# Window attention of a vision tower: the query and key product goes behind the projection, the value product changes its PSUM bank, and VectorE adds up rows earlier

## The reference, cut to what matters

```
xw  = windows of 8 x 8 = 64 positions, 64 channels each
qkv = xw @ qkv_w.T + qkv_b            # 8 heads of 8 channels
q, k = rope2(q), rope2(k)             # rotate pairs of channels by row and column
attn = softmax(q * 8 ** -0.5 @ k.T)   # 64 x 64, for each window and head
h = (attn @ v) @ proj_w.T + proj_b    # back in picture order
```

## Time and profile before

| | us |
|---|---|
| median of 3 runs | 1657.8 (1657.18 to 1657.87) |
| the profiled execution's own time | 1655.28 |
| its span in the trace | 1653.5 |
| TensorE busy, whole span | 1506.6 (91%) |
| VectorE busy | 1201.7 (73%) |
| ScalarE busy | 1004.9 (61%) |
| GpSimd busy | 614.9 (37%) |
| 8x8 stage, first to last transposition of maxima (L693) | 29.85 to 294.24 |

### The profile page before, as it was taken

One profiled execution on the slowest core, in us unless ns is written; L12 is line 12 of the kernel. 1 busy time (PEld: TensorE's weight loads), 2 busy tenths in 40 slices (PEclk: granted clock), 3 DMA queues, 4 the chain that ended last, 5 costly groups with the idle time before them and its releaser, 6 DMA issues.

```text
span 1653.5 us, 85382 instructions
## 1 busy us (share of the span) xinstructions
PE 1506.6 (91%) x30734; PEld 1082.0 (65%) x30734; DVE 1201.7 (73%) x3605; ACT 1004.9 (61%) x1925; POOL 614.9 (37%) x926
## 2 busy tenths in 40 slices
PE   6999999789999999999857999999999999999996
PEld 4777777668888888777745656556565655656552
DVE  2566666458888888888647778787787777877872
ACT  2444444345555555455312788888888888888876
POOL 4352232356666666666532222222222222222210
PEclk9999999989999999999976999999999999999996
DMA  5322222144444444444411454555545455554543
GB/s 140 69 50 48 47 47 42 46 119 124 129 126 128 134 129 124 129 128 127 115 38 33 73 93 81 85 87 80 92 79 90 82 84 88 78 93 78 90 81 57
DMA packets 146868, 147.44 MB, mean 89 GB/s; under 512 B 54898, under 2 KB 102258, under 8 KB 146546
## 3 DMA queue, kind: packets, MB, share of 16 engines
q1 hardware_dynamic: 137922, 117.38, 37.7%
q10 hardware_dynamic: 8880, 29.16, 6.1%
HBM read 66.48 MB, written 16.99 MB: 50 GB/s over the span
## 4 chain that ended last, share of the span: by engine, by line
PE 77%; ACT 9%; issue 6%; SPq 3%; POOL 2%; DVE 1%; DMA 1%; ACTq 0%; POOLq 0%; DVEq 0%
PE ps_D L923 10%; PE ps_D L831 8%; PE ps_OT L850 5%; ACT prob L1227 4%; PE ps_AV L942 4%; PE ps_AV L858 4%; PE ps_D L706 3%; ACT prob L1125 3%; PE ps_D L827 3%; PE ps_J L1000 3%; PE ps_J L1034 2%; PE ps_OT L1010 2%; PE ps_J L985 2%; PE ps_J L1065 2%; PE ps_OT L784 2%
## 5 line engine op out<-in xcount | busy, mean ns | idle before, releaser
L1227 ACT ACTIVATE prob<-ps_D 128x1024 bf16<-128x1024 f32 x448 | 459.4, 1028 | 114.8 <-PE ps_D L923 114.3
L1197 ACT ACTIVATE prob<-ps_D 100x512 f32<-100x512 f32 x256 | 138.8, 594 | 102.8 <-PE ps_D L831 102.8
L577 POOL TENSOR_TENSOR tile_a<-q_st,q_mask 128x512 f32<-128x512 f32 x128 | 135.2, 1056 | 150.7 <-PE ps_D L831 140.1
L831 PE MATMUL ps_D<-tile_a,key_patch 64*100 64x128 f32 x2048 | 174.6, 290 | 0.0
L1388 DVE TENSOR_REDUCE m_sb<-ps_D 128x4 f32<-128x400 f32 x256 | 134.5, 565 | 25.5 <-PE ps_D L808 25.5
L1350 DVE TENSOR_REDUCE top<-ps_D 128x8 f32<-128x512 f32 x128 | 79.6, 683 | 95.8 <-PE ps_D L684 95.7
L551 POOL TENSOR_TENSOR rstd_bin<-veps_bin,minus_half 128x2 f32<-128x2 f32 x64 | 44.1, 689 | 263.0 <-DVE veps_bin L1288 263.0
L551 POOL TENSOR_TENSOR rstd_ret<-veps_ret,minus_half 128x2 f32<-128x2 f32 x64 | 47.3, 739 | 241.8 <-DVE veps_ret L1288 241.8
L831 PEld LDWEIGHTS ps_D<-tile_a,key_patch 64*100 64x100 f32 x2048 | 134.0, 167 | 0.0
L827 PE MATMUL ps_D<-mT,key_rows 64*100 64x128 bf16 x1024 | 119.7, 229 | 6.3 <-ACT prob L1197 4.6
L923 PE MATMUL ps_D<-tile_b,w_parts 64*64 64x256 bf16 x2048 | 104.3, 287 | 15.5 <-ACT prob L1227 11.8
(11 more groups left out here) (184 smaller groups left out, 3828.4 us busy)
## 6 DMA issues: line engine op xcount, KB each, us to landing
tile_a<-xg SPq DMA_DIRECT2D x192, 128.0 KB, 4.5
tile_b<-xg SPq DMA_DIRECT2D x192, 128.0 KB, 4.5
key_st<-k_d SPq DMA_DIRECT2D x128, 162.0 KB, 3.1
tile_b<-v_d ACTq DMA_DIRECT2D x128, 120.0 KB
tile_b<-v_d ACTq DMA_DIRECT2D x64, 160.0 KB
w_exp<-experts SPq DMA_DIRECT2D x64, 129.0 KB, 2.3
xT<-in_x SPq DMA_DIRECT2D x32, 256.0 KB, 2.7
tile_a<-rot SPq DMA_DIRECT2D x256, 16.0 KB
```

Of the source, the lines that this page charges most:

```text
L577: gp.tensor_tensor(q_block[:, par, :].rearrange("c (p h q) -> c p h q", h=NH, q=NQ)[:, own, :, :], q_st[:, par, :].rearrange("c (p a q) -> ...
L831: mm = pe.matmul(s_loc[x][0:NKL, u * P:(u + 1) * P], key_patch[rows_of(x), par, at * NKL:(at + 1) * NKL], q_block[rows_of(x), par, at * P: ...
L1197: act.activation(prob1[0:NKL, 2 * g + x, :], s_loc[x][0:NKL, :], ACT.Exp).then_inc(T2["exp_done"], 1)
L1227: act.activation(sgn[:, k % 4, :], unit(k, par)[:, :], ACT.Sign).then_inc(BN["sign"], 1)
```

## The change

Four edits, all in the 8x8 stage:

- TensorE issues `tok_qk(i + 2)` behind `tok_project(i - 1)`, where it was ahead of `tok_scores(i)`.
- ScalarE issues `tok_sin(i + 2)` behind the four exponentials, where it was ahead of them.
- The values are made in columns 256 to 511 of bank OT, which the projection uses too, and no longer in bank T. With that the waits change: `tok_qk` no longer waits for `v_sb`. `tok_v` waits for `h_done` (VectorE's read of OT) in place of `cos_mul`. `tok_project` waits for `v_sb` (ScalarE's read of OT) too.
- VectorE issues `tok_rows(i - 1)` right behind `tok_normalize(i - 1)`, where it was behind the reductions.

```diff
             def tok_qk(...):
                 pe.wait_ge(T1["sin_in"], times(i))
-                pe.wait_ge(T1["v_sb"], times((i - 1) * 4))
             def tok_v(i, par):
                 pe.wait_ge(T1["v_sb"], times(i * 4))
-                pe.wait_ge(T1["cos_mul"], times(i + 2, NT))
+                pe.wait_ge(T1["h_done"], times(i - 1))
...
-                            at = (p * 2 + ab) * 32
-                            mm = pe.matmul(bank["T"][rows_of(e), at:at + 32], ...)
+                            at = 256 + (p * 2 + ab) * 32
+                            mm = pe.matmul(bank["OT"][rows_of(e), at:at + 32], ...)
             def tok_project(i):
                 pe.wait_ge(T1["attn_out"], times(i + 1))
+                pe.wait_ge(T1["v_sb"], times((min(i + 2, NT) if isinstance(i, int) else i + 2) * 4))
                 pe.wait_ge(T1["h_done"], times(i))
...
                 tok_top(i)
-                if not last or i + 2 < NT:
-                    tok_qk(i + 2, j + 1, par)
                 tok_scores(i, par)
                 if not last or i:
                     tok_project(i - 1)
+                if not last or i + 2 < NT:
+                    tok_qk(i + 2, j + 1, par)
...
             def tok(j, par):                          # ScalarE
-                if not last or i + 2 < NT:
-                    tok_sin(i + 2)
                 act.wait_ge(T1["av_done"], times(i))
                 act.wait_ge(T1["scores"], times(i + 1))
                 for n in range(4):
                     act.activation(prob1[:, n, :], s_tok[n][:, :], ACT.Exp).then_inc(T1["exp_done"], 1)
+                if not last or i + 2 < NT:
+                    tok_sin(i + 2)
...
                     tok_normalize(i - 1)              # VectorE
+                if not last or i:
+                    tok_rows(i - 1)
                 if not last or i + 2 < NT:
                     tok_rope(i + 2, par)
                 if not last or i + 1 < NT:
                     tok_max(i + 1)
-                if not last or i:
-                    tok_rows(i - 1)
```

More of the change, by code:

```diff
@@ L669, in tok_v @@
                         for e in range(2):
-                            at = (p * 2 + ab) * 32
-                            mm = pe.matmul(bank["T"][rows_of(e), at:at + 32], xT[rows_of(e), par, window(ab, p)], w_v1[rows_of(e), 32 * e:32 * (e + 1)],
+                            at = 256 + (p * 2 + ab) * 32
+                            mm = pe.matmul(bank["OT"][rows_of(e), at:at + 32], xT[rows_of(e), par, window(ab, p)], w_v1[rows_of(e), 32 * e:32 * (e + 1)],
                                            start=True, stop=True)
@@ L1105, in tok_v @@
                         act.activation(v_tok[par][rows_of(e), :, ab, :, at:at + HD],
-                                       bank["T"][rows_of(e), 0:256].rearrange("k (p s h d) -> k p s h d", p=4, s=2, d=HD)[:, :, ab, :, :], ACT.Copy).then_inc(T1["v_sb"], 1)
+                                       bank["OT"][rows_of(e), 256:512].rearrange("k (p s h d) -> k p s h d", p=4, s=2, d=HD)[:, :, ab, :, :], ACT.Copy).then_inc(T1["v_sb"], 1)
             def tok_sin(i):
```

## The result

| | before | after |
|---|---|---|
| median of the runs | 1657.74 (4 runs) | 1711.27 (4 runs, 1706.41 to 1716.79) |
| ratio, 95% interval | | 1.0296 (1.0261 to 1.033) |
| span of the profiled execution | 1653.5 | 1704.6 |
| first top (L693 before, L692 after) | 29.85 | 31.25 |
| top 7 | 93.57 | 101.70 |

The kernel is 3.0% slower. I had forecast 1680, slower, and a range up to 1702: the direction was right, the size less than half, and the time lies 9 us above the range. Of the 51.1 us between the spans, 1.4 are lost ahead of the first top, 6.7 until top 7, 40.8 in the 24 steps to top 31, and 2.2 behind them. So the loss is where I put it, and the question is why a step takes 10.06 and not 9.2. The profiled execution took 1706.4, the least of the four; the other three had a mean granted clock of 0.938 to 0.943, against 0.954 in this one.

What follows compares the result with a forecast made beforehand. TensorE's list and VectorE's chain were taken to bound steps of 8.36 us almost together. Late keys make it 9.2: +20.1 over 24 steps, +2.2 head, 1655.3 to 1677.6, plus 2.5 for the median: 1680, range 1664 to 1702.

Steps and rivals of the forecast that it cites:

- The copy of the maxima: Between top and scores: ScalarE's copy loses its cover, scores start at 0.77, 0.47 us of new idle time, step 8.68.
- The keys: Rotation and key transfers start later, so the second half of the maxima's products waits until 16.0; two steps take 18.4.
- The landing: From the eighth key issue's start to TensorE going on: 2.2 us, read from tile 0 only.
- The sum: 24 steps of 9.2 against 200.7 before: +20.1; with +2.2 for the head +22.3, so 1677.6, median 1680.
- The first rival: Keys late and the clock falls as well, in 10 of 24 steps at 1.9 us: 1699; chance 0.22.
- the step that fell before: Step 4 before the change: idle 1.07 and 0.57 came ahead of a 1.2 GHz stretch; one fall priced at 1.9.
- about 0.75 in each step: TensorE's stall for late keys ahead of the second half of the maxima's products, paid in full in every step.
- other steps of the head kept their clock: In the stage's first steps, an idle 1 us left the clock up; cited against the rival with clock falls.
- The head of the stage: Steps until tile 7, with constant loads between the keys in SyncE's queue: top 7 at 95.8, +2.2 us.
- Bank and rows at nothing: Values in the projection's bank and rows earlier cost nothing; the query and key product covers VectorE's addition, else 0.7 a step.
- Only the exposed copy: Rival: only the maxima's copy is exposed, keys in time, steps of 8.68 to 8.90: 1666 to 1671; chance 0.16.
- TensorE's list decides: Rival: reductions end 0.4 sooner, keys in time, steps of 8.40 on average: 1655 to 1658; chance 0.08.

Runs made afterwards that it cites:

- e2: Changed kernel with four key transfers per tile in place of eight (keys of every second head left out, output not the reference's): 1687.2 us, before 1659.1.
- e5: Changed kernel with half of the key transfers and one filler matmul on each side of the transposition of the maxima: 1662.1 us, before 1660.6.
- e10: Changed kernel with the last four key transfers of a tile issued by GpSimd and a filler matmul on each side of the transposition: 1663.4 us, before 1662.9.
- e3: Changed kernel with tok_sin, ScalarE's copy of bank J1, between the second and third exponential: 1688.8 us, before 1659.1.
- e6: Changed kernel, all keys, with three filler matmuls between the halves of the maxima's products and one on each side of the transposition: 1676.5 us, before 1660.6.
- e9: Changed kernel, all keys, with one filler matmul on each side of the transposition and none between the product halves: 1705.8 us, before 1662.9.
- e7: Changed kernel with query and key product and tok_sin moved back; values stay in bank OT, rows behind the division: 1691.9 us, before 1660.6.
- e8: Kernel before with only the addition of rows moved behind the division: 1735.1 us, ratio 1.0445.
- e4: Changed kernel with six filler matmuls between the two halves of the maxima's products: 1691.4 us, before 1659.1.
- e11: Kernel before, nothing of the change, with its 30 constant loads spread over ten steps in place of six: 1652.95 us, ratio 0.9951.

## Why the prediction was wrong

**The direction and its two mechanisms were right.** *The copy of the maxima*: scores start 0.76 after top (162.50 to 163.26; forecast 0.77), and a step with no late keys takes 8.69 (forecast 8.68, e2 and e5). *The keys*: counted from the transposition two steps back, at 153.78, GpSimd starts at 5.93 (forecast 5.82), SyncE at 8.78 (8.71), the second half of the maxima's products at 16.34 (16.0). The landing took 2.44 from the eighth issue (167.68 to 170.12), 0.24 more than my one row gave. e10 shows that issuing the keys faster removes the wait in 21 of 24 steps.

**The step that failed is the clock.** The sum priced every step at full clock, so the falls stood in it at nothing. Between tops 7 and 31 the changed kernel has ten falls, one of them over 10 us long (212 to 222, clock 0.50), and a mean granted clock of 0.92. From the second half to the next top it takes 3.72 in place of 2.4, the transposition 0.46 in place of 0.30, and the pair is 20.2: 18.4 + 0.3 for the landing + 1.5 for the clock. The average step splits as follows:

- exposed copy: 8.69 - 8.36 = 0.33, times 24 is 7.9 us (e5);
- late keys at full clock: a pair of 16.34 + 2.4 = 18.7, so 9.35 - 8.69 = 0.66, times 24 is 15.8 (the forecast had 9.2, 3.6 less);
- clock: 10.06 - 9.35 = 0.71, times 24 is 17.0. Together 1.70 a step, 40.8 us.

The 9.35 is worked out, and two runs bear it out: e3 has pairs of 18.6 without and 20.0 with a fall in one execution, and e6, with the clock held up, has 19.0, of which 0.3 are its filler.

From 1680 to 1711 the terms are: 17.0 for the clock, 3.6 for the landing, 4.5 for the head, 1.4 ahead of the first top, 2.2 behind top 31, and 2.4 since the median lies 4.9 above the profiled execution and not 2.5. The clock alone would have left the time at 1697, in the range; it is more than half of the miss. The first rival, late keys with ten falls at 1.9 us, had 19 us for the clock in place of 17.0, in as many falls; its 1699 is too low by the other terms. So that rival, with its chance of 0.22, is what happened.

**Why I under-priced it.** I compared lengths: idle times of 0.47 and 0.75 against 1.07 and 0.57 in the step that fell before. Three things were wrong with that. Once the clock falls, the wait for keys doesn't spread over both steps, as I wrote ("about 0.75 in each step"): tiles of even and odd number have chains of their own, one of them takes the whole wait, 1.61, and the other finds its keys in place. (At full clock it did spread, 1.08 and 0.57 in e9.) And the 0.47 behind the transposition has a twin ahead of it, since VectorE's chain now ends 0.4 behind TensorE's list. I had that in the numbers (8.31 against 8.68) and didn't count it as idle time. e2 shows that these two alone, 0.92 in 1.2 us, can be enough.

And the kernel before had a second fall, which I missed: I wrote that other steps of the head kept their clock with an idle 1 us. In its first step TensorE is idle for 0.43 and 0.55 ahead of the two halves of the maxima's products (34.79 and 35.76). These are its windows over the idle time and over what follows:

```profile
34.00:36.00 2.00, 1.02 (x45) 0.80 (x42) 0.67 (x2) 1.95 (x7) 0.94 (x1) 1.00 0.46 131
36.00:38.00 2.00, 2.00 (x63) 1.44 (x55) 1.81 (x4) 0.51 (x2) 0.00 (x0) 0.70 0.66 155
38.00:40.00 2.00, 2.00 (x47) 1.59 (x41) 0.80 (x1) 0.28 (x1) 0.00 (x0) 0.50 0.18 21
```

So idle times as short as the new step's already stood ahead of a fall in the trace of the kernel before.

By the Trainium skill, TensorE: Matmul & The Clock Gate, "A second HAM failure mode", short idle times between groups make the clock go back and forth. I had given the rows of the steady part more weight than this rule; e2 agrees with the rule, in its later steps with a fall in each.

**The head of the stage** was forecast at +2.2 and is +6.7. There are falls in it too: steps 1, 3 and 5 of after take 12.0, 12.6 and 11.6, and the mean granted clock from the first top to top 7 is 0.90 (0.95 before). That doesn't settle it: e6 has no fall there and still lost 5.3, with one step of 12.5 in which TensorE is idle for 1.76 without a releaser in the trace. How much of the 4.5 is the clock stays open.

**Bank and rows at nothing**: right for the change as a whole, since the values have no idle time ahead of them after. It was right for the stated reason, the cover by the query and key product: without it the loop of e7 is 23.2 us longer than before. I had not seen that the old bank needs the old order of VectorE (e8).

**The rivals.** "Only the exposed copy" did not happen here, but is what most steps of e5 and e10 run like. Their totals lie 1 us over the kernel before by one execution, less than the 8 that the steps say: both gained 5.5 to 6 us ahead of top 7, which the changed kernel doesn't have. "TensorE's list decides" did not happen: with keys in time VectorE's chain set the step at 8.7 in e2, e5 and e10.

## What to carry to other kernels

When an instruction moves, count what it covered and what it feeds through the slowest queue, over as many steps as the chain takes: here the product for tile i + 2 feeds rotation, eight issues of 0.73 us and a landing, and two steps have to hold it all. Then add up TensorE's new idle times where they lie close together, the ones ahead of an instruction and behind it too. Look for every place of the trace where as much idle time came close together, and read the granted clock behind it. Here 0.92 us in each step brought the clock down in 20 steps of e2 and left it up in the 11 before. If rows speak for both, give the fall a price in the sum (here 0.71 of the 1.70 us that a step lost), and if it matters, test it with a few matmuls that compute nothing. And compare stage by stage: in single executions the same work behind the stage came out up to 13 us apart from that of the kernel before.

## What the runs showed of the hardware

- Two idle times of 0.46 around one transposition, with nothing else idle, left the clock at full speed in steps 0 to 10 and then went along with a fall in every one of the next 20 (e2); with both idle times filled in part there was none in the loop (e5). The steps before and after the first fall are the same work; why the state lasts was not tried.
- Filler matmuls made the 24 steps of the changed kernel 5.2 us (e4) and 13.6 us (e6) shorter, and those of e2 29.9 us (e5). In e9, with the stall for the keys left open, they gained nothing.
- A 128x128 f32 matmul takes 0.27 us on TensorE at full clock, as two entries of the trace (12 entries for six, 1.60 us).
- A key transfer of 16 KB takes 0.73 us to issue on SyncE. Four issues on GpSimd took 2.26 us, shorter than SyncE's 2.90 for four, and started 0.6 later (e10).
- The kernel before has a median of 1657.7, 1660.6 or 1662.9 on different chips, and single executions of it went from 1651.9 to 1670.1, so only comparisons on one chip are used for e8 and e11.
